# A decoder block: seven quarter products in the FFN, sorted tokens scattered as fp16 halves, GpSimd's rsqrts in another order

## The reference, cut to what matters

```python
x = x + attn(layernorm(x))          # linear attention, 16 heads: elu features, kv, silu(u) gate, Wo
x = x + experts(layernorm(x))       # each token by its id to one of 4 experts: (silu(h Wg^T) * (h Wu^T)) Wd^T
# third part, for 4 x 512 tokens, d = 512, e = 2048, wu, wg, wd = ternary_quant(W): values -s, 0, s
up   = einsum('bsd,ed->bse', layernorm(x), wu)
gate = einsum('bsd,ed->bse', layernorm(x), wg)
x = x + einsum('bse,de->bsd', silu(up) * gate, wd)
```

## Time and profile before

| | us |
|---|---|
| median of 3 runs (lowest, highest) | 746.62 (746.39, 747.16) |
| the profiled execution | 747.43 |
| its span, first to last instruction | 745.7 |
| busy: PE, DVE, ACT, POOL | 715.1, 377.0, 273.2, 125.0 |

### The profile page before, as it was taken

One profiled execution on the slowest core, in us unless ns is written; L12 is line 12 of the kernel. 1 busy time (PEld: TensorE's weight loads), 2 busy tenths in 40 slices (PEclk: granted clock), 3 DMA queues, 4 the chain that ended last, 5 costly groups with the idle time before them and its releaser, 6 DMA issues.

```text
span 745.7 us, 11582 instructions
## 1 busy us (share of the span) xinstructions
PE 715.1 (96%) x3979; PEld 380.9 (51%) x4008; DVE 377.0 (51%) x622; ACT 273.2 (37%) x426; POOL 125.0 (17%) x186
## 2 busy tenths in 40 slices
PE   8999999999999988999998999999999999999996
PEld 5556557557565655666544444444444444444442
DVE  5667766866856654664464343353434433342233
ACT  4365545536537243344222322222222222222221
POOL 3113624314315600000010000020000200020002
PEclk8999999999999999999999999999999999999999
DMA  8914026025127289531011000020001200010001
GB/s 226 367 59 168 1 113 208 18 94 204 41 114 282 89 298 334 198 113 30 15 30 30 14 15 14 1 71 14 14 14 15 70 14 14 14 56 1 0 1 56
DMA packets 45606, 64.00 MB, mean 86 GB/s; under 512 B 22784, under 2 KB 22784, under 8 KB 44544
## 3 DMA queue, kind: packets, MB, share of 16 engines
q1 hardware_dynamic: 41728, 50.89, 21.7%
q0 software_dynamic: 3840, 12.59, 4.5%
HBM read 46.69 MB, written 12.59 MB: 79 GB/s over the span
## 4 chain that ended last, share of the span: by engine, by line
PE 79%; DVE 7%; DMA 4%; issue 3%; ACT 3%; POOL 2%; SPq 1%; POOLq 0%; DVEq 0%; ACTq 0%
PE bank L1340 29%; PE bank L1070 26%; PE bank L1350 13%; PE bank L1063 4%; DVE region L761 2%; PE bank L1227 2%; PE bank L1263 2%; PE bank L1241 2%; DMA n<-sorted_tokens 2%; DVE late L757 1%; DMA sorted_residual<-rows,pos 1%; DMA w_att<-nrm 1%; DMA stage<-in_L_attn_Wv_dram 1%; SPq L188 1%; POOL sorted_residual L324 1%
## 5 line engine op out<-in xcount | busy, mean ns | idle before, releaser
L1340 PE MATMUL bank<-w_att,region 128*128 128x512 f16 (+1 forms) x1024 | 231.1, 379 | 2.7 <-DMA w_att<-nrm 2.7
L1340 PEld LDWEIGHTS bank<-w_att,region 128*128 (+1 forms) x1024 | 100.1, 98 | 123.7 <-issue 3.4
L1033 DVE SCALAR_TENSOR_TENSOR tmp<-tmp,hk,bank 128x512 f32<-128x512 f32 x64 | 47.8, 747 | 155.9 <-PE bank L1340 155.5
L1350 PE MATMUL bank<-region,tmpA 128*128 (+1 forms) x452 | 111.3, 379 | 1.5
L1070 PE MATMUL bank<-late,w_att 128*128 128x512 f16 x384 | 87.2, 383 | 1.1 <-DVE region L804 1.0
L609 ACT ACTIVATE tmp<-bank,qs 128x512 f32<-128x512 f32 x64 | 44.0, 687 | 116.7 <-PE bank L1340 116.7
L307 POOL TENSOR_SCALAR ve<-mv 128x1 f32<-128x1 f32 (+1 forms) x37 | 9.2, 248 | 455.8 <-DVE mv L971 340.5
L616 ACT ACTIVATE tmpA<-tmp 128x512 f16<-128x512 f32 x62 | 39.0, 629 | 120.2 <-DVE tmp L1033 120.2
L1350 PEld LDWEIGHTS bank<-region,tmpA 128*128 128x128 f16 x480 | 46.8, 98 | 56.8 <-DVE stage L1017 0.9
L1037 DVE TENSOR_TENSOR tmpA<-tmp,tmpA 128x512 f16<-128x512 f32 x62 | 43.0, 693 | 44.1 <-ACT tmpA L616 44.1
L1070 PEld LDWEIGHTS bank<-late,w_att 128*128 128x128 f16 x384 | 37.6, 99 | 44.1 <-DVE region L804 2.0
(11 more groups left out here) (144 smaller groups left out, 809.7 us busy)
## 6 DMA issues: line engine op xcount, KB each, us to landing
stage<-in_L_ffn_W_up_dram SPq DMA_DIRECT2D x8, 1024.0 KB, 5.9
stage<-in_L_ffn_W_gate_dram SPq DMA_DIRECT2D x8, 1024.0 KB, 5.3
rows<-sorted_residual SPq DMA_DIRECT2D x4, 1026.0 KB, 10.1
stage<-in_ctx_dram SPq DMA_DIRECT2D x4, 1024.0 KB, 6.6
stage<-in_L_ffn_W_down_dram SPq DMA_DIRECT2D x4, 1024.0 KB, 7.2
nrm<-in_L_ffn_W_down_dram SPq DMA_DIRECT2D x4, 1024.0 KB, 7.3
n<-sorted_tokens SPq DMA_DIRECT2D x16, 256.0 KB, 5.1
rows<-in_x_dram SPq DMA_DIRECT2D x1, 3072.0 KB, 19.3
```

The costliest lines, as they stand in the source:

```text
L1033: dve.scalar_tensor_tensor(out=h32, in0=sil, scalar=hk[:, 0:1], in1=gate_ps[:, :], op0=ALU.mult, op1=ALU.mult).then_inc(s["hid_mul"], 1)
L1340: mm = pe.matmul(dst, w[:, bass.ds(cf_c, 1), k * P:(k + 1) * P].rearrange("p a n -> p (a n)"), x3T[:, bass.ds(b, 1), i, k].rearrange("p a ...
L1350: mm = pe.matmul(ffy_ps[t][:, :], hid[:, parity, i, t * P:(t + 1) * P], tern[2][:, bass.ds(c, 1)].rearrange("p a n -> p (a n)"), start=(st ...
```

## The change

**FFN.** Up and gate of a group become a product of two-by-two blocks by seven quarter products (Winograd's form): tokens of a batch in halves (tiles 0, 1 and 2, 3), d in halves, hidden columns in a top and a bottom half. VectorE builds the seven operands of x from the norm (`x3_sums`), VectorE and GpSimd build sums of the ternary weights (`up_sum`, `gate_sum`). A part is 8 matmuls of 256 columns; VectorE adds the parts out of four rotating banks. GpSimd now makes the low halves of the hidden values (`hid_lo`) and of x (`x3_lo`, 128 x 1792), and SP turns hi and lo of two tile pairs per batch, 14 blocks each.

**Sorting.** The second norm goes to `region`; ScalarE and VectorE split it at once (`n2_hi`, `n2_lo`), the scatter sends both halves, and the load of a sorted tile is a DMA transpose straight into `x3T`. `xs_transpose`, `xs_hi`, `xs_lo` are gone, and z has two banks.

**Orders.** The o rsqrt of a batch stands ahead of the scatters, the scatter of batch 2 behind the last o rsqrts, and the last second-norm rsqrts ahead of most of the last scatters. `keep_busy` between two unit transposes is 150 matmuls instead of 100. The loops of the FFN are written out.

The core of the diff, in the order SP, GpSimd, ScalarE (attention, then the gate of a group), VectorE (the gate of a group; `gate_of` adds a part out of its bank, `gated` multiplies with silu of up) and TensorE (a part, the gate of a group, the batches):

```diff
         def sorted_tile(i):
-            sp.dma_start(xs_slot[i % 3], xs_v[:, i]).then_inc(s[f"xs_in{i % 3}"], 16)
+            sp.dma_start_transpose(
+                out=x3T[:, i // T, :, :, (i % T) * P:(i % T + 1) * P].rearrange("p i k s -> p (i k) s"),
+                in_=xs_v[i]).then_inc(s[f"xs_in{i % 4}"], 16)
...
+        def x3_turned(b, p):
+            for h in range(2):
+                sp.wait_ge(s["x3_lo" if h else "x3_hi"], 2 * b + p + 1)
+                sp.dma_start_transpose(out=x3S_in[b % 2][:, h, :, p * P:(p + 1) * P], in_=x3h[:, h]).then_inc(
+                    s["x3_lo_in" if h else "x3_hi_in"], 16)
...
         def scatter(b, t):
-            pool.wait_ge(s["x2_norm"], T * b + t + 1)
-            pool.indirect_dma_start(xs_dram, row_of(T * b + t), n2[:, t], None).then_inc(s["scattered"], 16)
+            pool.wait_ge(s["n2_lo"], T * b + t + 1)
+            pool.indirect_dma_start(xs_dram, row_of(T * b + t), n2h[:, t].rearrange("p h d -> p (h d)"), None).then_inc(s["scattered"], 16)
...
+        def x3_lo(k):
+            pool.wait_ge(s["x3_hi"], k + 1)
+            if k > 0:
+                pool.wait_ge(s["x3_lo_in"], 16 * k)
+            pool.tensor_tensor(x3h[:, 1], x3_flat[:, 0:7 * H], x3h[:, 0], ALU.subtract).then_inc(s["x3_lo"], 1)
...
+        def group(b, t):
+            n = T * b + t
+            if n < NT - 1:
+                hid_lo(n, 0, 0, g11)
+                hid_lo(n, 1, 3, g22)
+            if b + 1 < B and t % 2 == 0:
+                third_rsqrt(2 * b + 2 + t // 2)
+            if b + 1 < B and t % 2 == 1:
+                x3_lo(2 * b + 2 + t // 2)
+            if n < NT - 1:
+                hid_lo(n, 2, 1, g21)
+                hid_lo(n, 3, 2, g12)
+            if t == 0 and b > 0:
+                send_out(b - 1)
...
             first_norm(b + 1)
             if first:
                 magnitudes(b, 1)
+            else:
+                for t in range(T):
+                    n2_hi(b - 1, t)
             o_copies(b)
...
+            act.wait_ge(s["gate_mm"], 7 * n + 1)
+            act.activation(g22, wk_ps[(14 * n + 7) % 4][:, :], ACT.Copy).then_inc(s["gate_copy"], 1)
+            hid_hi(n, 0, 0, g11)
+            if b + 1 < B and t % 2 == 1:
+                x3_hi(2 * b + 2 + t // 2)
+            hid_hi(n, 1, 3, g22)
+            hid_hi(n, 2, 1, g21)
...
+            gate_of(g12, 1, g22)
+            gate_of(g11, 2, g22)
...
+            gate_of(g21, 3, g12)
...
+            gated(n, 0, u11, g11)
...
+            gate_of(g22, 4, g21)
+            gate_of(g12, 4, g12)
...
+            gate_of(g21, 5, g21)
+            gated(n, 1, u22, g22)
...
+            gate_of(g12, 6, g12)
...
+            gated(n, 2, u21, g21)
...
+            gated(n, 3, u12, g12)
...
+        def part(bank, w, c, slot, m):
+            for q in range(2):
+                for h in range(2):
+                    for k in range(2):
+                        mm = pe.matmul(wk_ps[bank][:, q * H:(q + 1) * H], w[:, c + q, k * P:(k + 1) * P],
+                                       x3S_part[slot][:, h, m, k], start=(h == 0 and k == 0), stop=(h == 1 and k == 1))
...
+            gate(0, A11, 0)
+            gate(1, S2, 5)
+            gate(2, A12, 1)
+            gate(3, S3, 4)
+            downs_before(2)
+            gate(4, S1, 3)
+            gate(5, A22, 6)
+            gate(6, S4, 2)
+            downs_before(3)
...
+        for b in range(B):
+            pe.wait_ge(s["x3_hi_in"], 32 * b + 32)
+            pe.wait_ge(s["x3_lo_in"], 32 * b + 32)
+            for t in range(T):
+                group(b, t)
```

More of the change, by code:

```diff
@@ L547, in _ @@
         batch(0, True, False)
-        with act.Fori(1, B - 1) as b:
+        for b in range(1, B - 1):
             batch(b, False, False)
@@ L554, in _ @@
         o_copies(B - 1)
+        for t in range(T):
+            n2_hi(B - 2, t)
         magnitudes(B - 1, 1)
@@ L620, in batch3, with silu @@
-        def batch3(b, first, nxt):
-            group(b, 0, first, nxt)
-            with act.Fori(1, T if nxt else T - 1) as t:
-                group(b, t, False, nxt)
-            if not nxt:
-                group(b, T - 1, False, False, True)
-        batch3(0, True, True)
-        with act.Fori(1, B - 1) as b:
-            batch3(b, False, True)
-        batch3(B - 1, False, False)
+        def silu(n, q, dst, src):
+            act.activation(dst, src, ACT.Silu, scale=qs[:, 0:1]).then_inc(s["up_act"], 1)
@@ L633, in _ @@
+        for b in range(B):
+            for t in range(T):
+                group(b, t)
+        hid_hi(NT - 1, 3, 2, g12)
     @block.vector
@@ L875, in batch @@
                 routing_positions()
+            elif not last:
+                for t in range(T):
+                    n2_lo(b - 1, t)
             if last:
@@ L888, in batch @@
                     aggregate(1, t, "o_stat", T * b + T, "o_aggr")
-            if not first:
-                dve.wait_ge(s["scattered"], 16 * T * b)
+            if last:
+                for t in range(T):
+                    n2_lo(b - 1, t)
         def signs_of(g, j):
@@ L1006, in _, with finish @@
+            if i == 12:
+                up_sum(S3[0], A11[0], A21[0], ALU.subtract, 1)
+            if i == 15:
+                up_sum(S2[0], S1[0], A11[0], ALU.subtract, 2)
+            if i == 16:
+                up_sum(S4[0], A12[0], S2[0], ALU.subtract, 3)
         for i in range(STEPS):
             expert_step(i)
[L1008 to L1016 removed]
+        def finish(b, tiles, parts):
+            for t, part in zip(tiles, parts):
+                dve.wait_ge(s["down_mm"], part)
+                if b > 0:
+                    dve.wait_ge(s[f"out_done{t}"], 16 * b)
@@ L1058, in _ @@
+        for b in range(B):
+            for t in range(T):
+                group(b, t)
+        finish(B - 1, range(T), [4 * NT - 3 + i for i in range(T)])
     @block.tensor
@@ new lines, in _ @@
+        pe.wait_ge(s["up_sums"], 4)
+        pe.wait_ge(s["gate_sums"], 4)
+        for b in range(B):
+            pe.wait_ge(s["x3_hi_in"], 32 * b + 32)
+            pe.wait_ge(s["x3_lo_in"], 32 * b + 32)
+            for t in range(T):
+                group(b, t)
+        c = C // 2 - 2
+        for t, (first, then) in enumerate((((0, 1), (1, 3)), ((0, 1), (1, 3)), ((3, 3), (2, 4)), ((3, 3), (2, 4)))):
+            for u, lo in (first, then):
+                pe.wait_ge(s["hid_lo"], 4 * NT - 4 + lo)
+                mm = down(c + C // 2 if u in (1, 3) else c, u, (t,), False, u == then[0])
+            mm.then_inc(s["down_mm"], 1)
```

478 lines of the change are left out of this document (271 added, 207 removed).

## The result

The changed kernel takes 764.11 us (median of 4 runs, 761.87 to 765.73) beside 746.89 for the kernel before on the same chip: a ratio of 1.0226, interval 1.0196 to 1.0255. It is slower, as forecast, but by 17 us and not by 3. The profiled execution is the fastest of its four: 761.87 us, span 760.1, mean granted clock 0.977; the other three had 0.968 to 0.970. In that span the loss against before (745.7) is 14.4 us.

The account below looks back on a forecast made before the run. TensorE was taken as the bound in late expert steps and FFN. FFN +12.1 us (-25.3 products, +36.9 boundaries, +0.5 rest) and -9.0 before it sum to +3.1: 750.5 profiled, 749.7 median, range 741 to 761.

Parts of the forecast that it names:

- Products: FFN: 256-column matmuls at 0.109 us make a group 19.14 us, 1.58 less; 16 groups give -25.3 us.
- VectorE keeping up inside a batch: FFN inside a batch: VectorE has 15.3 us of work per 19.1 us group, so no wait is charged.
- the boundary: FFN batch starts: TensorE waits 10.3 us for the last low half, plus 2.0 of clock; three cost +36.9 us.
- put the fourth z at 288.9: Expert stage: the fourth product with a sorted tile starts at 288.9 instead of 289.50 us, -0.6.
- the gate unit's chain: Before the fourth sorted product: gate weight unit 4.9 us later, at 283.9, then sign passes, unit transposes, th and issue.
- the stage's end: Attention stage: ScalarE's token copies cost +3.3 us over batches 1 and 2, and +0.4 in batch 3.
- the last tokens: End of attention: subtractions around VectorE's final norm make the last half ready at 256.1, scatter before at 254.95: +1.2 us.
- The o copies: Attention batches 1 and 2: ScalarE's fp16 token copies delay the copies of o; TensorE waits 1.65 us, +3.3 for both.
- I count 3.1 of the 3.7 as gained, since four sums of 2048 columns on VectorE come in: End of expert stage: 22.5 us of work in 26.25; the old x3 chain's rest mostly goes, -3.1 us.
- GpSimd's four sums: Late expert steps: four weight sums and two x3_lo take GpSimd 25 to 40 us; nine steps give 50.
- GpSimd slowed by VectorE: Rival: slower GpSimd lengthens boundaries and makes third quarters late; FFN about +23, total 760 us; 756 to 768, chance 0.15.
- the third quarters: Slowed-GpSimd rival, batch's second group: third quarter comes after 17.4 us, 1.4 us late for TensorE in three groups.

Follow-up runs that it names:

- the seven kernels with this attention code: Seven kernels measured here with the changed kernel's attention code unaltered; their attention stages end between 253.30 and 254.98 us, the changed kernel's own the latest.
- the run with the earlier group: Changed kernel with the second tile pair's x3 work for the next batch done one group of four chunks earlier; 727.63 us, ratio 0.9739.

## Why the prediction was right and wrong

**Right: the FFN.** Products (0.109 us for 256 columns, group 19.14), VectorE keeping up inside a batch, and the boundary were as worked out: 9.5 us of wait beside 10.3, of which x3_lo gives 0.6 (4.0 for 4.6) and the transpose 0.2; 2.35 us of clock beside 2.0. The estimate of 3.9 us for x3_lo that the forecast worked out from the Trainium skill's "GPSIMD Engine Reference", section "Elementwise — side-by-side cycle accounting", was nearer to the measured 4.01 than the value taken. The FFN's +10.7 beside +12.1 needs no other cause, and the run with the earlier group gives back 34.4 of the boundaries' 35.6 us.

**Wrong: "put the fourth z at 288.9".** The step took the gate unit's chain and left out the sorted tiles' own: its own 4.9 us of delay on z0 (262.71) and three steps of 8.21 - 0.44 us would have given 290.9, later than the weight unit allowed. Measured, z0 was 7.7 late, of which 5.0 at the stage's end (3.7 forecast; 3.3 to 5.0 over the seven kernels with this attention code), 2.2 in the last tokens (1.2 forecast) and 0.5 from there on; and behind its wait of 2.62 us TensorE took 4.45 us instead of 2.76 for z0, the granted clock at 0.50 from 271.4 on. The fourth came 4.3 us later than forecast. The o copies themselves were rightly seen, 1.3 us a batch instead of 1.65; what else the stage lost, 0.7 to 2.4 us in smaller waits, is not settled.

**Wrong: "I count 3.1 of the 3.7 as gained, since four sums of 2048 columns on VectorE come in".** This is the step that failed most: the stretch from z10 to the FFN came out 8.2 us longer than forecast, of the 14.4 us between 749.7 and 764.1 (the rest: the fourth z 4.3, z3 to z10 0.2, the median 3.0, the FFN -1.4). It counted the work and not what is queued behind it on VectorE: h_lo stood behind x3_normalise and x3_sums (2.2 us). It gave GpSimd's four sums room (25 to 40 us in 50) and did not ask what they do to VectorE's normalisations, which lasted 2.94 and 3.63 us (2.2 us more, 48.8 to 46.7 in the table above). And it had no term for TensorE's reads ahead of z13 and z16 (2.7 us). What is left of 8.8 us is 1.7.

**The rivals.** The time landed 4 us above the one of GpSimd slowed by VectorE, but not through its mechanism: the third quarters were not late, x3_lo was near its best rate, and the slowing of note was VectorE by GpSimd. Of the distance to the forecast, 3 us lie between the profiled run and the median, which is 2.2 above it (at the lower mean clock named above) where 0.8 below was taken over from before.

## What to carry to other kernels

Where work is moved into a stage with slack, list for each moved instruction what stands behind it in its engine's order and who waits for that; the busy shares did not show it here. Where two chains could release a point, work out both and take the later. A loss that an edit does not remove may hide behind another one that ends at the same place: take them out together before calling either harmless, and look for the change's own cure in its order (here a group earlier, and 3.5% faster than before).

## What the runs showed of the hardware

- VectorE's normalisation (one input and two scalars per row) of 128x512 fp32 took 0.54 us alone (in the kernel before, and where the sums were kept apart), and 2.29, 2.99 and 4.27 us when a GpSimd sum of 2048 columns was running: each time until 0.2 to 0.3 us behind that sum's end. The Trainium skill, "SBUF — State Buffer", "Who interferes with whom", says that such VectorE instructions can take the ports shared with GpSimd and that the second to come is blocked fully; these runs agree. The forecast used that section for instructions with two inputs alone. GpSimd was slower in turn: a subtraction of 512 columns took 1.53 us beside VectorE's multiplications and 1.16 without.
- TensorE's reads of a register's value ahead of a product came with idle time of 0.15 to 0.25 us in most steps and 1.2 to 1.8 ahead of z13 and z16, both times just behind the issue of the half tiles' transposes (365.12 and 386.21, for z13 at 367.98 and z16 at 389.78). That the reads are what TensorE waits for is shown by moving them; that the transposes slow them is only argued from where they lie.
- A transposing load of three sorted tiles from DRAM took 4.3 to 6.25 us from its issue to z0; what makes it longer no run shows.
- The same kind of wait did not always cost clock. Behind the wait for the first sorted tile the granted clock stayed at 1.00 and z0 took 2.76 us in six profiles (waits of 2.33 to 3.50 us); in seven it fell to 0.50 and z0 took 4.11 to 5.30 us (waits of 2.62 to 5.02 us). The forecast had read the price from one such row.
